# Two-stage cross attention on one core: G of the first batch completed between the two row maxima, and a reordered last pair in which GpSimd makes three low parts

## The reference

```python
# layer 0
q, k, v = x @ w_q.T, ctx @ w_k.T, ctx @ w_v.T
x1 = x + alpha * (softmax(q @ k.T / sqrt(512)) @ v) @ w_o.T
# layer 1, x_2 = ctx; batch by batch, C = 256 channels, N = 512 positions
theta = theta_w @ x1 + theta_b          # 128 x 512
phi   = phi_w @ ctx + phi_b             # 128 x 512
g     = g_w @ ctx + g_b                 # 128 x 512
y     = ((theta.T @ phi) / 512 @ g.T).T
out   = batchnorm(w_w @ y + w_b) + x1
```

## Time and profile before

| | |
|---|---|
| median of three executions | 395.88 us |
| profiled execution | 395.43 us |
| its span, first to last instruction | 393.6 us |
| TensorE busy | 385.4 us, 98% of the span |
| VectorE busy | 291.4 us, 74% |
| ScalarE busy | 190.8 us, 48% |
| GpSimd busy | 1.8 us |
| mean granted TensorE clock | 0.997 |

### The profile page before, as it was taken

One profiled execution on the slowest core, in us unless ns is written; L12 is line 12 of the kernel. 1 busy time (PEld: TensorE's weight loads), 2 busy tenths in 40 slices (PEclk: granted clock), 3 DMA queues, 4 the chain that ended last, 5 costly groups with the idle time before them and its releaser, 6 DMA issues.

```text
span 393.6 us, 5814 instructions
## 1 busy us (share of the span) xinstructions
PE 385.4 (98%) x1967; PEld 328.6 (83%) x1967; DVE 291.4 (74%) x567; ACT 190.8 (48%) x385; POOL 1.8 (0%) x7
## 2 busy tenths in 40 slices
PE   8999999999999999999999999999999999999985
PEld 5888988889888988889888988889888988889863
DVE  5896559875698568876689567876698667876775
ACT  3464735652547335563448235563448244572441
POOL 1000000000000000000000000000000000000000
PEclk9999999999999999999999999999999999999998
DMA  8985554157650965248750966348650875016612
GB/s 244 374 311 226 151 150 113 70 171 257 203 171 2 343 176 180 100 142 285 206 167 0 312 194 185 108 122 292 185 201 0 283 219 177 13 53 188 196 45 107
DMA packets 55803, 68.13 MB, mean 173 GB/s; under 512 B 4592, under 2 KB 46320, under 8 KB 52720
## 3 DMA queue, kind: packets, MB, share of 16 engines
q1 hardware_dynamic: 55792, 67.99, 53.3%
HBM read 49.09 MB, written 18.87 MB: 173 GB/s over the span
## 4 chain that ended last, share of the span: by engine, by line
PE 88%; DVE 4%; DMA 3%; ACT 2%; SPq 1%; issue 1%; DVEq 0%; POOL 0%; POOLq 0%
PE bank L303 22%; PE bank L304 21%; PE bank L305 21%; PE bank L362 6%; PE bank L332 6%; PE bank L350 3%; PE bank L352 3%; PE bank L351 3%; DMA gram_moved<-gram_blocks 2%; SPq L216 1%; PE bank L319 1%; DVE xb L816 1%; DMA moved<-blocks 1%; ACT c_raw L513 1%; DVE x_lo L664 1%
## 5 line engine op out<-in xcount | busy, mean ns | idle before, releaser
L303 PE MATMUL bank<-ov_hi,c_sides 128*128 128x512 f32 x128 | 50.2, 392 | 0.0
L304 PE MATMUL bank<-ov_lo,c_sides 128*128 128x512 f32 x128 | 49.9, 390 | 0.0
L305 PE MATMUL bank<-ov_hi,c_sides 128*128 128x512 f32 x128 | 49.9, 390 | 0.0
L305 PE MATMUL bank<-c_sides,qk_lo 128*128 128x512 f32 x128 | 49.8, 389 | 0.0
L303 PE MATMUL bank<-c_sides,qk_hi 128*128 128x512 f32 x128 | 49.8, 389 | 0.0
L304 PE MATMUL bank<-c_sides,qk_hi 128*128 128x512 f32 x128 | 49.8, 389 | 0.0
L352 PE MATMUL bank<-tT_hi,xT_lo 128*128 128x256 f32 x128 | 36.2, 283 | 0.0
L351 PE MATMUL bank<-tT_lo,xT_hi 128*128 128x256 f32 x128 | 36.2, 283 | 0.0
L350 PE MATMUL bank<-tT_hi,xT_hi 128*128 128x256 f32 x128 | 36.2, 283 | 0.0
L558 ACT ACTIVATE probs<-bank,neg_max 128x256 f32<-128x256 f32 x32 | 14.9, 471 | 39.5 <-DVE neg_max L751 39.5
L493 ACT ACTIVATE x_hi<-xb 128x512 fp32r<-128x512 f32 x32 | 19.7, 632 | 28.1 <-DVE xb L816 28.0
(11 more groups left out here) (129 smaller groups left out, 860.6 us busy)
## 6 DMA issues: line engine op xcount, KB each, us to landing
cT_raw<-ctx_t SPq DMA_DIRECT2D x8, 1024.0 KB, 5.0
xT_raw<-x_t SPq DMA_DIRECT2D x8, 1024.0 KB, 8.4
c_raw<-ctx_n SPq DMA_DIRECT2D x8, 1024.0 KB, 6.1
xb<-x SPq DMA_DIRECT2D x16, 512.0 KB, 4.9
out<-xb SPq DMA_DIRECT2D x15, 512.0 KB, 3.5
gram_moved<-gram_blocks SPq DMA_DIRECT2D x16, 256.0 KB, 6.1
gram_blocks<-gram_moved SPq DMA_DIRECT2D x64, 64.0 KB, 2.0
moved<-blocks SPq DMA_DIRECT2D x16, 256.0 KB, 2.7
```

What stands on the lines that cost most here:

```text
L303: pe.matmul(dst, ahi, bhi, start=(k == 0), stop=False)
L304: pe.matmul(dst, ahi, blo, start=False, stop=False)
L305: mm = pe.matmul(dst, alo, bhi, start=False, stop=(k == k_tiles - 1))
```

## The change

The edits are these.

- VectorE, every pair: `gram_close(0)` now stands between `turn_squares(0)` and `row_maxima(1)`, and `gram_part(0)` between `row_maxima(1)` and `turn_squares(1)`. `gram_close(1)` comes right after the inverted sums (and the low part of `wg` in the first pair).
- ScalarE, every pair: `gram_part(0)` stands between the exponentials of the two batches.
- Last pair, TensorE: both `phi_gram` precede `values(1, 0)`. After the deltas come `w_g_phi(0)`, `w_g_phi(1)`, `theta_rows(0)`, `theta_rows(1)`; before, `theta_rows(0)` was first.
- Last pair, VectorE: `phi_squares` come before `pT_part(0)`, `u_rows` comes right after the first of four `x1_row`, and `t1_rows`, `t1_part` precede `theta_part(0)`. ScalarE's order follows.
- Last pair, GpSimd: it makes the low parts of x1 of the first batch (two) and of `u`. TensorE waits for them on two new semaphores.

```diff
@@ TensorE
-                values(1, 0)
+                if not last:
+                    values(1, 0)
                 for b in range(2):
                     pe.wait_ge(gram_lo, two[b + 1])
                     phi_gram(b)
+                if last:
+                    values(1, 0)
                 values(1, 1)
...
                 if last:
-                    pe.wait_ge(x1_lo, four[2])
-                    theta_rows(0)
-                    pe.wait_ge(u_lo, p + 1)
+                    pe.wait_ge(u_last_lo, 1)
                     pe.wait_ge(x1_made, four[4])
                     w_g_phi(0)
                     w_g_phi(1)
-                    pe.wait_ge(x1_lo, four[4])
+                    pe.wait_ge(x1_last_lo, KL)
+                    theta_rows(0)
+                    pe.wait_ge(x1_lo, four[2])
                     theta_rows(1)
@@ ScalarE
                 exp(0)
+                gram_part(0)
                 exp(1)
...
                 vo_part(0, 0)
-                gram_part(0)
                 gram_part(1)
...
-                for lt in range(KL):
-                    x1_part(0, lt)
+                x1_part(0, 0)
                 if last:
                     u_part()
+                x1_part(0, 1)
                 for lt in range(KL):
                     x1_part(1, lt)
                 if last:
-                    theta_part(0)
                     t1_part(0)
                     t1_part(1)
+                    theta_part(0)
                     theta_part(1)
@@ VectorE
                 row_maxima(0)
                 turn_squares(0)
+                gram_close(0)
                 row_maxima(1)
+                gram_part(0)
                 turn_squares(1)
                 for b in range(2):
                     invert_sums(b)
                 if first:
                     lo(wg, wg_hi, 1, (every,), bank[WG_BANK][:].rearrange("p (k l) -> p k l", k=KS), wg_lo)
-                gram_close(0)
+                gram_close(1)
                 vo_part(0, 0)
-                gram_part(0)
-                gram_close(1)
                 gram_part(1)
                 vo_part(0, 1)
+                if last:
+                    phi_squares(0)
+                    phi_squares(1)
                 pT_part(0)
                 vo_part(1, 0)
-                phi_squares(0)
-                phi_squares(1)
+                if not last:
+                    phi_squares(0)
+                    phi_squares(1)
...
                 if last:
+                    x1_row(0, 0)
                     u_rows()
-                    u_part()
...
+                    x1_row(0, 1)
+                    x1_row(1, 0)
+                    x1_row(1, 1)
+                    lo(x1, x1_hi, four[3], (every, 1, 0), xb[:, 1, 0], x1_lo)
+                    lo(x1, x1_hi, four[4], (every, 1, 1), xb[:, 1, 1], x1_lo)
                     for b in range(2):
                         t1_rows(b)
                     for b in range(2):
                         t1_part(b)
+                    theta_part(0)
                     theta_part(1)
@@ GpSimd
+            pool.wait_ge(x1_hi, 2 * KL * (PAIRS - 1) + 1)
+            pool.tensor_tensor(x1[1][:, 0, 0], xb[:, 0, 0], x1[0][:, 0, 0].bitcast(F32),
+                               ALU.subtract).then_inc(x1_last_lo, 1)
+            pool.wait_ge(u_hi, PAIRS)
+            pool.tensor_tensor(u[1][:].rearrange("p x (q a) -> p x q a", q=BLOCKS),
+                               phi_blocks[:].rearrange("p q x a -> p x q a"),
+                               u[0][:].rearrange("p x (q a) -> p x q a", q=BLOCKS).bitcast(F32),
+                               ALU.subtract).then_inc(u_last_lo, 1)
+            pool.wait_ge(x1_hi, 2 * KL * (PAIRS - 1) + 2)
+            pool.tensor_tensor(x1[1][:, 0, 1], xb[:, 0, 1], x1[0][:, 0, 1].bitcast(F32),
+                               ALU.subtract).then_inc(x1_last_lo, 1)
```

More of the change, by code:

```diff
@@ L452, in pair @@
                     pe.wait_ge(theta_lo, two[2])
-                    for ct in range(KL):
-                        output(1, ct)
+                    output(1, 0)
+                    output(1, 1)
                     return
```

39 lines of the change are left out of this document (18 added, 21 removed).

## The result

The changed kernel takes **404.87 us** (median of 6 executions, 401.94 to 406.03); the kernel before took 395.97 in the same set (395.79 to 397.61). The ratio is 1.0205, 95% interval 1.0161 to 1.0248: slower, and by more than the range of the forecast (397.6 to 402.2) allowed. The profiled execution took 403.73 us, its span 401.9, which is 8.3 us longer than before. Its mean granted TensorE clock is 0.991, and the six executions order by it: 401.94 us at 0.996, 403.73 and 403.84 at 0.991, 405.89 to 406.03 at 0.985 to 0.987.

A forecast was written before the change was run, and what follows sets the result against it. TensorE was taken to bound the kernel, busy 385.4 of 393.6 us. First pair +2.6, loop +0.3 and last pair +1.3 sum to +4.2 us, 399.6 for the profiled execution and 400.1 as median; range 397.6 to 402.2.

The forecast's parts named there:

- First pair, +3.0: First pair: TensorE newly waits 3.0 us for the low part of `wg` before `values(1, 0)`, until 56.95.
- The 0.43: First pair: the old 0.43 us wait for `u` disappears, giving that time back.
- Loop, +0.3: Pairs of the loop: one pair's squares come late, +0.3 us, with bounds 0 to 1.8.
- The clock, a rival at 0.15: First pair: the 3.0 us wait halves the clock for nine products, 2.0 us more, 402.1 in all; chance 0.15.
- The wait that the forecast itself put behind the last deltas: Last pair: TensorE waits some 3 us after the deltas, before `w_g_phi`.
- Landing of phi G, start of x + 6.3 us: Last pair: phi G's squares land behind the megabyte of x, 6.3 us after its loads start, at 375.9.
- nothing of the wait is gained: Last pair: `w_g_phi` starts at 382.5, where before it started at 382.58.
- The rival of short transfers: Last pair: phi G's squares land in 2.3 us, the tail gives 1.1 back, 397.7 in all; chance 0.12.
- `theta_rows(0)` behind the wait, +1.36: Last pair: `theta_rows(0)`, which filled 1.36 us before the wait for `u`, now stands behind it.
- GpSimd's subtraction, 1.4: Last pair: GpSimd takes 1.4 us per subtraction, bounds 0.5 and 2.9.
- The port, a rival at 0.10: Last pair: VectorE's and GpSimd's SBUF reads exclude each other, `theta_rows(0)` comes 0.7 us later, 400.8; chance 0.10.
- the likeliest case: Whole kernel: the main forecast of 400.1 us, chance 0.56, spanning 399.4 to 401.5 alone.

The follow-up runs named there:

- g_only: Kernel before with only the new place of the first batch's G, in every pair on VectorE and ScalarE; 401.34 us, ratio 1.012.
- wg_ahead: The change with both parts of `wg` made ahead of the additions that wait for the squares, in the first pair; 401.11 us, ratio 1.011.
- both_busy: The change with 12 products of zeros ahead of the first pair's wait for `wg_lo`, 17 ahead of the last pair's for `u`; 400.71 us.
- x_early: The change, new G order in last pair only, loads of x there ahead of the fetches of the probabilities; 397.13 us, ratio 1.0017.
- phi_before_x: The change, new G order in last pair only, phi G squares sent ahead of the loads of x; 397.42 us, ratio 1.0023.
- tail_old: The change, new G order in last pair only, phi G early but that pair's remaining order as before, no GpSimd; 396.96 us, ratio 1.0008.
- before_busy: Kernel before with eight products of zeros ahead of its 1.9 us wait for `u` in the last pair; 395.75 us, ratio 0.9978.
- busy_first: The change with twelve products of zeros ahead of the first pair's wait for `wg_lo`; 401.24 us, ratio 1.0141.

## Why the prediction was wrong

The sign and the chain of waits were right; the size was not, since the sum had nothing for the clock. The forecast was +4.2 us in the profiled execution, the measurement +8.3: 3.2 of the difference is the clock, 0.8 the landing of phi G, 0.1 the loop.

- **First pair, +3.0: right.** The replay put the low part of `wg` ready at 56.95, and TensorE started at 56.98. g_only shows that the edit of G makes it, wg_ahead that the cause is VectorE's queue: the same landing costs 0.9 us when `wg` is ahead of it. The 0.43 came back as forecast.
- **Loop, +0.3: right in kind, and in size for the profiled execution.** It measured 0.4, and the wait that shows, of the weight load in the second pair, is for `u_lo`, whose thin cover the forecast had named. Over the six traces with G early in the loop it was 0.4 to 1.0, so 0.3 was low, though within the bounds of 0 to 1.8.
- **The clock, a rival at 0.15, was the step that failed.** It was asked only whether the wait in the first pair brings the clock down, at 2.0 us; that part measured 1.7. The wait that the forecast itself put behind the last deltas, some 3 us, was not asked the same question, and cost 1.5 more. The argument against the rival was a single case, 1.92 us without a fall. That was one execution of a wait behind which the clock falls in some executions and not in others: waits of 1.94, 1.96 and 2.00 us were followed by the fall (x_early, phi_before_x, tail_old), and before_busy gains 0.2% by filling the 1.9 us of the kernel before. With the clock held (both_busy) the change measures 400.71, the forecast was 400.1. Both waits should have had the fall in the sum: 1.7 + 1.5 more than 400.1, which is 403.3. The trace of before held a warning too, in its last product:

  ```profile
  388.56 0.40 PE L305 MATMUL bank<-theta_hi,t_lo 128*128 128x512 f32 x1
  ```

  The clock was at a mean of 0.80 from 391 to 392, so TensorE had stood idle for 2 to 3 us when it fell, no longer than in the forecast's own two waits.
- **Landing of phi G, start of x + 6.3 us: mis-sized.** It took 7.2, so `u_rows`, and `w_g_phi` behind them, were 0.8 us later than forecast. In the eight other traces with the squares leaving right behind x it took 6.7 to 7.3, so this was no single late landing. That it hangs on the loads of x and not on its own leaving was right, and so was "nothing of the wait is gained". The rival of short transfers described what happens with nothing in front: 2.56 us in phi_before_x, against 2.3 in the first pair.
- **`theta_rows(0)` behind the wait, +1.36: right.**
- **GpSimd's subtraction, 1.4: right**, at 1.28. The bounds of 0.5 and 2.9 were far wider than needed; the range for the time should have held them even so, since by the forecast's own terms 2.9 us costs 3.0 us more, which is 403.1 and outside it. The Trainium skill (GPSIMD Engine Reference, Elementwise — side-by-side cycle accounting) has about 2.6 cycles per element for a GpSimd instruction with two inputs; at its 1.2 GHz that is an estimate of 1.1 us for 512 elements, without what it takes to start one. The trace's 1.28 lies 0.2 above it.
- **The port, a rival at 0.10: half right.** The Trainium skill (SBUF — State Buffer, Who interferes with whom) has a VectorE instruction with two SBUF inputs and a GpSimd instruction that reads SBUF exclude each other. The traces agree in the pair of rows above, 2 subtractions in 2.32 to 2.34 us against 3 in 1.89. But VectorE was the one held up, by about 1.1 us, not GpSimd, and TensorE was busy with `w_g_phi` and `theta_rows(0)` meanwhile, so none of it is seen in the span.
- **The range.** Its upper end of 402.2 is the clock rival alone (402.1) and almost nothing else; a fall of the clock together with a late landing or a costlier loop was not in it. The lower end of the likeliest case, 399.4, doesn't come out of its terms either: 395.88 + 2.6 + 0 + 1.3 is 399.8.
- **Left open.** The median of the change lies 1.1 us above its profiled execution, where the forecast allowed 0.45. The three slowest executions had a lower mean clock (0.985 to 0.987), which fits longer stretches at the lower level. The trace of g_only shows one such stretch, from about 56 to over 62 us behind a single wait, but of the change no such execution was traced. Why 1.92 us brings the clock down in one execution and not in the next, and why 3.23 us did not in busy_first, was not settled.

## What to carry to other kernels

Price a new wait on TensorE as the wait plus slow products behind it, with a chance rather than a certainty (here they came behind most waits of 1.9 to 4.1 us, not all), and ask this of every wait that the forecast itself predicts, not only of the one that the edit creates. Work that waits for a round trip through memory should stand on its engine behind all that TensorE asks for sooner. And before work is moved up so that its transfer leaves earlier, look at what stands in front of it on the queue: here the order of two transfers was worth 2.5 us, and leaving some 1.6 us earlier behind the megabyte of x was worth nothing.

## What the runs showed of the hardware that was not expected

- When the clock falls is not tied to TensorE's restart. In the change it showed 1.00 to the end of the wait, then 0.59 and 0.50; in g_only it was at 0.50 for the last microsecond of a wait of the same length (3.0 us); at the end of the kernel before it fell with TensorE idle, a mean of 0.80 from 391 to 392 us, while at the end of the change it still showed 1.00 four us behind the last product.
- What it costs is not fixed either. In the traces of the change and of g_only TensorE ran as many slow products as 8 to 12 of 512 columns at 0.43 us (those of 256 columns at 0.21). Behind a wait of 3.23 us in busy_first it ran none, and behind 1.9 us the clock fell in some executions and not in others.
- Products of zeros in a wait hold the clock, so added work makes a kernel faster: ratio 1.0205 to 1.0098 for the change, and 0.9978 (0.9965 to 0.9991) for the kernel before.
- A send of the phi squares that left 1.9 us sooner behind the loads of x (0.94 us after their start instead of 2.85) landed 0.9 us later, counted from that start: 7.2 instead of 6.3.
- A GpSimd subtraction of 128 x 512 held up VectorE's of the same kind for almost its whole length, and was not slowed itself (1.28 and 1.29 us with and without VectorE's beside it).
